# 64-row key transposes, and the first half of the attention step in another order

## The chip, the cores and the metric

The kernel runs on one core of a Trainium2 chip. The metric is the time of one execution on the device, in microseconds (us). The core's engines are TensorE (PE, its weight loads PEld), VectorE (DVE), ScalarE (ACT), GpSimd (POOL) and SyncE (SP), which here only issues DMAs. Each engine runs its own list of instructions in order, and semaphores tie the lists together.

## The reference

`x` and `ctx_4096` are (32, 64, 512): 32 batches, 64 channels, 512 positions. A linear cross attention comes first, then a feed-forward layer with 4-bit weights.

```python
qh = einsum('bcn,oc->bon', layernorm(x), Wq)    # 8 heads of 64
kh = einsum('bcn,oc->bon', ctx, Wk)
vh = einsum('bcn,oc->bon', ctx, Wv)
qh = softmax(qh, axis=-2) * SCALE               # over a head's 64 features
kh = softmax(kh, axis=-1)                       # over the 512 positions
context = einsum('bhdn,bhen->bhde', kh, vh)
out = einsum('bhde,bhdn->bhen', context, qh)
out = einsum('bcn,oc->bon', out.reshape(b, 512, -1), Wo) + bo
x = x + tanh(g_xattn) * (out / max(norm(out, axis=1), 1e-12) * g * sqrt(64))
x = x + tanh(g_ffn) * ffn(layernorm(x))         # gate, up and down products
```

## The kernel before

The attention works on pairs of batches: 16 pairs, two times 64 channels on the 128 partitions. The loop is a software pipeline of steps p = 0 to 17. In step p the logits and exponentials of pair p are made ("project"), the denominators and the context of pair p-1 ("combine"), and the output, its norm and the residual of pair p-2 ("residual"). Steps 0, 1, 16 and 17 do a part of this; 16 and 17 are the drain, where the feed-forward's input is transposed too. The steps are written out by hand, one list for each engine, and semaphores are counted by pair. The feed-forward layer (lines from 1097 on) comes after it and isn't touched.

TensorE's list in a full step has two halves. The first: `t_logits(t)` (query logits with n on the partitions, only for the row maxima, L625), `k_logits(t)` (L646), `denominators` (L679), `output` (L663), `context(t)` (L691: the transposed context input ctxT times the transposed key exponentials ekT, into the bank small[0]), `squared_norms` (L702), `q_max_rows` (transposes of the row maxima, L715) and `fold_context` (L726, also into small[0]). The second half is four rounds t = 0 to 3 of `spread_reciprocals(t)` (L743), `q_logits(t)` (L761 three times, then L763, which subtracts the maxima; all into k_pair) and `k_transposed(t)` (L776: 128 positions of all key exponentials ek are transposed into act_pair). `ctx_transposed` (L786) stands in round 0, `spread_inverse_norm` (L797) in round 2.

Who waits for whom around the change:

- ScalarE empties the banks in order. In a round it does the exponential of the query logits (L493, semaphore q_exp), then the copy of the transposed keys to ekT (L489, kt_evac). `q_logits(t)` waits for q_exp of round t-1, since both use k_pair; `k_transposed(t)` waits for kt_evac of round t-1.
- In the first half ScalarE does the key exponentials (L484, two for each t, after DVE's minimum L982), y and ysq (L501, L502), xs_hi (L452), ss_rows (L510), kctxT (L506, the context product out of small[0]; semaphore a_evac), qmax_rows (L555) and ctxT (L563; ct_evac).
- `fold_context` waits for a_evac. VectorE does the maxima (L979, L982), the reciprocals L991, and in the second half the products eq (L987).

A matmul's stationary operand fills rows x columns of the array. A row of the profile shows this as "64*128" or "128*128", and the moving operand behind it. "pair" is any of dve_pair, k_pair and act_pair, "small" either of small[0] and small[1].

## Time and profile before

| what | value |
|---|---|
| time, median of 3 runs | 786.22 us (785.8 to 786.3) |
| the profiled execution's own time | 788.89 us |
| its span | 787.1 us |
| TensorE, VectorE, ScalarE, GpSimd busy | 93%, 76%, 55%, 23% |
| mean granted TensorE clock | 0.974 of full speed |

The profiled execution took 2.67 us more than the median of the runs, of which 1.8 us lie outside its span. Times in the rows are counted from the start of the span. A row of the timeline gives a start, a duration up to the end of the last instruction merged into it, the engine, the line, and how many were merged; an idle time before it and its releaser follow in brackets. Matmuls are pipelined, so the duration of a row reaches beyond the start of the next one, and start to start is what a row costs. The attention steps fill the first 459 us or so, the feed-forward layer the rest.

### The profile page before, as it was taken

The numbers are of one execution on the slowest core, as the hardware profiler recorded it, in microseconds if no ns is written. First come the engines' busy times: TensorE is split into PE (matmuls) and PEld (weight loads), VectorE is DVE, ScalarE is ACT, GpSimd is POOL, SyncE is SP. The second block draws the span as 40 slices with busy tenths as digits, with TensorE's granted clock in tenths as the row PEclk, the third lists the DMA queues.
The fourth block names the chain that finished last, engine by engine and source line by source line (L and its number), as shares of the span: only waits on it lengthen the run. The fifth ranks groups of instructions, "written<-read, shape, count | busy, mean of one in ns | idle before, by whom it ended". The sixth has DMA issues, their size and how long they took to land. (4 is left out here: it accounts for less than half of the span.)

```text
span 787.1 us, 13752 instructions
## 1 busy us (share of the span) xinstructions
PE 732.0 (93%) x4551; PEld 395.1 (50%) x4551; DVE 594.7 (76%) x806; ACT 436.3 (55%) x764; POOL 179.5 (23%) x317
## 2 busy tenths in 40 slices
PE   4789999999999999999999754799999999999997
PEld 3445554565456545654565331254555455554555
DVE  6356878887888788778876463699988878877885
ACT  3657776677667767776776421354443344445333
POOL 5221222222222222222241112112121111111221
PEclk9999999999999999999999956799999999999999
DMA  3003303330233012202200000200001000100101
GB/s 102 28 5 84 81 13 85 85 85 11 80 82 84 19 58 69 71 16 61 70 20 7 4 4 1 75 1 0 1 2 40 15 0 13 40 0 0 40 13 54
DMA packets 29195, 29.89 MB, mean 38 GB/s; under 512 B 18628, under 2 KB 18756, under 8 KB 29036
## 3 DMA queue, kind: packets, MB, share of 16 engines
q1 hardware_dynamic: 26972, 28.85, 13.3%
q10 hardware_dynamic: 2192, 0.66, 0.3%
q8 instruction: 16, 0.26, 0.1%
q14 instruction: 15, 0.12, 0.1%
HBM read 23.49 MB, written 4.23 MB: 35 GB/s over the span
## 5 line engine op out<-in xcount | busy, mean ns | idle before, releaser
L1303 DVE SCALAR_TENSOR_TENSOR acc<-ffn_bank,scale_T,acc 128x512 f32<-128x512 f32 (+1 forms) x264 | 186.6, 747 | 39.6 <-PE ffn_bank L1256 34.1
L1255 PE MATMUL ffn_bank<-ek,w_gu 128*128 (+3 forms) x352 | 137.8, 392 | 3.0 <-PEq L90 1.8
L1256 PE MATMUL ffn_bank<-ekT,w_gu 128*128 (+3 forms) x352 | 134.1, 381 | 0.0
L987 DVE TENSOR_TENSOR eq<-eq,pair 128x1024 f32<-128x1024 f32 x64 | 78.1, 1221 | 65.8 <-PE pair L743 65.8
L1163 POOL TENSOR_TENSOR in_lo<-inter,in_hi 128x512 fp32r<-128x512 f32 (+1 forms) x44 | 56.4, 1283 | 229.8 <-ACT in_hi L1202 229.8
L1195 ACT ACTIVATE act_gate<-acc 128x512 f32<-128x512 f32 (+1 forms) x44 | 27.7, 631 | 144.3 <-DVE acc L1303 144.3
L484 ACT ACTIVATE ek<-pair,kneg 128x512 f32<-128x512 f32 x128 | 86.7, 686 | 8.2 <-DVE kneg L982 7.8
L1272 PE MATMUL ffn_bank<-wd_hi,in_hi 128*128 128x512 f32 (+1 forms) x176 | 86.7, 531 | 0.4 <-DVE wd_lo L1336 0.4
L979 DVE TENSOR_REDUCE qmax<-pair 128x16 f32<-128x1024 f32 x64 | 77.6, 1212 | 12.4 <-PE pair L625 12.2
L1272 PE MATMUL ffn_bank<-wd_lo,in_hi 128*128 128x512 f32 (+1 forms) x176 | 86.7, 531 | 0.0
L493 ACT ACTIVATE eq<-pair 128x1024 f32<-128x1024 f32 x64 | 65.7, 1026 | 30.5 <-PE pair L763 30.5
L1255 PEld LDWEIGHTS ffn_bank<-ek,w_gu 128*128 128x128 bf16 (+1 forms) x352 | 34.8, 99 | 91.8 <-issue 48.3
L982 DVE TENSOR_REDUCE kneg<-pair 128x2 f32<-128x1024 f32 x64 | 77.8, 1215 | 1.4 <-PE pair L646 1.4
L1272 PE MATMUL ffn_bank<-wd_hi,in_lo 128*128 128x512 f32 (+1 forms) x176 | 77.5, 479 | 0.1
L776 PE MATMUL pair<-ident,ek 128*128 128x128 f32 x512 | 70.8, 282 | 0.0
L776 PEld LDWEIGHTS pair<-ident,ek 128*128 128x128 f32 x512 | 55.5, 142 | 23.6 <-issue 16.9
L489 ACT ACTIVATE ekT<-pair 128x1024 f32<-128x1024 f32 x64 | 65.7, 1027 | 0.9 <-PE pair L776 0.9
L691 PE MATMUL small<-ekT,ctxT 128*64 128x512 f32 x256 | 62.4, 610 | 0.8 <-ACT den L497 0.8
L663 PE MATMUL small<-eq,fold 128*64 128x512 f32 x256 | 60.7, 618 | 2.1 <-ACT ekT L489 1.1
L1187 ACT ACTIVATE acc<-ffn_bank,scale_T 128x512 f32<-128x512 f32 (+1 forms) x88 | 58.5, 684 | 2.6
L349 POOL TENSOR_TENSOR rn_sq<-ss_max,minus_half 128x8 f32<-128x8 f32 x16 | 26.6, 1663 | 114.8 <-DVE ss_max L1025 114.8
L359 POOL TENSOR_TENSOR cs_lo<-ctx_raw,cs_hi 128x512 fp32r<-128x512 f32 x16 | 20.5, 1280 | 129.8 <-ACT cs_hi L448 129.7
(138 smaller groups left out, 1147.0 us busy)
## 6 DMA issues: line engine op xcount, KB each, us to landing
xall<-in_x SPq DMA_DIRECT2D x16, 256.0 KB, 2.7
ctx_raw<-in_ctx SPq DMA_DIRECT2D x16, 256.0 KB, 2.9
out_x<-xall SPq DMA_DIRECT2D x16, 256.0 KB, 2.0
zero<-zeros_plus SPq DMA_DIRECT2D x8, 344.0 KB, 4.3
packed<-in_L_ffn_gate_qweight SPq DMA_DIRECT2D x4, 688.0 KB
packed<-in_L_ffn_up_qweight SPq DMA_DIRECT2D x4, 688.0 KB
packed<-in_L_ffn_down_qweight SPq DMA_DIRECT2D x10, 256.0 KB
d_scale<-in_L_ffn_down_scales SPq DMA_DIRECT2D x1, 1408.0 KB, 6.2
```

What stands on the lines that cost most here:

```text
L484: act.activation(ek[:, b, t, :], k_pairs[t % 2][:, b, :], ACT.Exp, bias=kneg[:, b, t:t + 1], scale=-1.0, accum_out=ksum[:, k_slot(b, t):k_ ...
L489: act.activation(ekT[:, t, :, :], act_pair[:, :, :], ACT.Copy).then_inc(kt_evac, 1)
L493: act.activation(eq[:, par, t, :, :], k_pair[:, :, :], ACT.Exp).then_inc(q_exp, 1)
L691: last = pe.matmul(small[0][half(b), :], ctxT[:, t, half(b)], ekT[:, t, b, :], start=(t == 0), stop=(t == NT - 1))
L776: last = pe.transpose(act_pair[:, b, ot * P:(ot + 1) * P], ek[:, b, ot, t * P:(t + 1) * P], ident[:, :])
L979: dve.tensor_reduce(qmax[:, t, :, 0:HEADS], dve_pair[:, :, :].rearrange("n b (h d) -> n b h d", d=DH), AX.X, ALU.max).then_inc(t_max, 1)
L982: dve.tensor_reduce(kneg[:, :, t], k_pairs[t % 2][:, :, :], AX.X, ALU.min).then_inc(k_max, 1)
L987: dve.tensor_tensor(e, e, dve_pair[:, :, :], ALU.mult).then_inc(q_norm, 1)
L1255: pe.matmul(gu_bank[job % 4][0:w, :], lhsT, xT_hi[:, g, rows], start=True, stop=False)
L1256: pe.matmul(gu_bank[job % 4][0:w, :], lhsT, xT_lo[:, g, rows], start=False, stop=True).then_inc(gu_mm, 1)
L1272: ins = pe.matmul(y_bank[t][:, :], left, right, start=(it == 0 and kind == 0), stop=(it == IT - 1 and kind == 2))
L1303: dve.scalar_tensor_tensor(out=acc[0:w, it % 3, m, :], in0=gu_bank[job % 4][0:w, :], scalar=scale_T[0:w, it, 4 * m + g:4 * m + g + 1], in1 ...
```

## The change

Four edits.

1. `k_transposed` no longer transposes eight blocks of 128 rows but sixteen of 64 rows, in eight pairs: rows 0 to 63 into bank 0 of act_pair, rows 64 to 127 into bank 1. ekT so has another order of columns, and `context` reads it in runs of 64 numbers. `spread_inverse_norm` uses 64 rows instead of 128.
2. On TensorE `context(0)` to `context(3)` stand together behind `k_logits(2)`; before, `t_logits(3)`, `k_logits(3)` and `squared_norms` stood between the two halves.
3. `ctx_transposed` moves from round 0 of the second half to just ahead of `q_max_rows`, and from bank small[1] to small[0]. It now waits for a_evac, and `fold_context` waits for ct_evac of the same step.
4. ScalarE's list follows: y and ysq behind the key exponentials of t = 1, ss_rows behind kctxT, and ctxT ahead of qmax_rows. The wait for the last key exponentials moves from `k_transposed(0)` to the last matmuls of `q_logits(0)`.

```diff
--- before.py
+++ after.py
@@ -539,18 +539,20 @@
                     denominators()
                 k_exp_tile(0, 0)
                 k_exp_tile(0, 1)
+                k_exp_tile(1, 0)
+                k_exp_tile(1, 1)
                 if residual:
                     outputs()
-                k_exp_tile(1, 0)
-                k_exp_tile(1, 1)
                 if not last:
                     x_high(p + 1, 1 - par)
-                if residual:
-                    squared_norms()
                 k_exp_tile(2, 0)
                 k_exp_tile(2, 1)
                 if combine:
                     context()
+                if residual:
+                    squared_norms()
+                act.wait_ge(ct_mm, p + 1)
+                act.activation(ctxT[:, :, :].rearrange("n t c -> n (t c)"), small[0][:, :], ACT.Copy).then_inc(ct_evac, 1)
                 act.wait_ge(qmaxT_mm, p + 1)
                 act.activation(qmax_rows[:, :], small[1][:, :], ACT.Copy).then_inc(qmaxT_evac, 1)
                 k_exp_tile(3, 0)
@@ -558,10 +560,6 @@
                 for t in range(NT):
                     q_exp_tile(t)
                     k_transposed(t)
-                    if t == 0:
-                        act.wait_ge(ct_mm, p + 1)
-                        act.activation(ctxT[:, :, :].rearrange("n t c -> n (t c)"), small[1][:, :],
-                                       ACT.Copy).then_inc(ct_evac, 1)
 
             def transposed(first, end):
 
@@ -656,7 +654,7 @@
                         if at_least(p, 3):
                             pe.wait_ge(yn_ready, r - 1)
                         if not drain or combine:
-                            pe.wait_ge(ct_evac, r + 1)
+                            pe.wait_ge(qmaxT_evac, r + 1)
                         else:
                             pe.wait_ge(ss_evac, r - 1)
                     for b in range(2):
@@ -673,6 +671,7 @@
                         pe.wait_ge(yn_ready, r - 1)
                     if isinstance(p, int) and p == 1:
                         pe.wait_ge(pool_consts, POOL_CONSTS)
+                        pe.wait_ge(ct_evac, 1)
                     for tt in range(2):
                         for grp in range(4):
                             b, t = grp // 2, 2 * (grp % 2) + tt
@@ -688,8 +687,9 @@
                         pe.wait_ge(ct_evac, r + 1)
                         pe.wait_ge(d_evac, r + 1)
                     for b in range(2):
-                        last = pe.matmul(small[0][half(b), :], ctxT[:, t, half(b)], ekT[:, t, b, :],
-                                         start=(t == 0), stop=(t == NT - 1))
+                        heads = ekT[:, t, :, b * OT * DH:(b + 1) * OT * DH].rearrange("n e (t d) -> n t e d", d=DH)
+                        last = pe.matmul(small[0][half(b), :].rearrange("c (t e d) -> c t e d", t=OT, e=2),
+                                         ctxT[:, t, half(b)], heads, start=(t == 0), stop=(t == NT - 1))
                     if t == NT - 1:
                         last.then_inc(a_mm, 1)
 
@@ -710,7 +710,7 @@
                     if residual:
                         pe.wait_ge(ss_evac, r)
                     elif combine:
-                        pe.wait_ge(ct_evac, r + 1)
+                        pe.wait_ge(qmaxT_evac, r + 1)
                     for t in range(NT):
                         last = pe.transpose(small[1][:, t * P:(t + 1) * P],
                                             qmax[:, t, :, :].rearrange("n b h -> n (b h)"), ident[:, :])
@@ -720,6 +720,8 @@
                     if not combine:
                         return
                     pe.wait_ge(a_evac, r + 1)
+                    if project:
+                        pe.wait_ge(ct_evac, p + 1)
                     for b in range(2):
                         for t in range(OT):
                             for e in range(2):
@@ -759,6 +761,8 @@
                     for n, (w, v) in enumerate(((wqT_hi, xs_hi), (wqT_lo, xs_hi), (wqT_hi, xs_lo))):
                         for b in range(2):
                             pe.matmul(k_pair[:, b, :], w[half(b), cols], v[half(b), par, :], start=(n == 0), stop=False)
+                    if t == 0:
+                        pe.wait_ge(k_exp, 8 * p + 8)
                     for b in range(2):
                         last = pe.matmul(k_pair[:, b, :], minus_spread[half(b), t, :], qmax_rows[half(b), :],
                                          start=False, stop=True)
@@ -767,23 +771,24 @@
                 def k_transposed(t):
                     if not project:
                         return
-                    if t == 0:
-                        pe.wait_ge(k_exp, 8 * p + 8)
-                    else:
+                    pe.wait_ge(pool_consts, 2)
+                    if t > 0:
                         pe.wait_ge(kt_evac, 4 * p + t)
-                    for b in range(2):
-                        for ot in range(OT):
-                            last = pe.transpose(act_pair[:, b, ot * P:(ot + 1) * P], ek[:, b, ot, t * P:(t + 1) * P],
-                                                ident[:, :])
+                    for slot in range(2 * OT):
+                        b, ot = divmod(slot, OT)
+                        for e in range(2):
+                            last = pe.transpose(act_pair[:, e, slot * DH:(slot + 1) * DH],
+                                                ek[half(e), b, ot, t * P:(t + 1) * P], ident[half(e), half(e)])
                     last.then_inc(kt_mm, 1)
 
                 def ctx_transposed():
                     if not project:
                         return
                     pe.wait_ge(loaded[par], 32 * (i + 1))
-                    pe.wait_ge(qmaxT_evac, p + 1)
+                    if combine:
+                        pe.wait_ge(a_evac, r + 1)
                     for t in range(NT):
-                        last = pe.transpose(small[1][:, t * P:(t + 1) * P], ctx_raw[:, par, t * P:(t + 1) * P], ident[:, :])
+                        last = pe.transpose(small[0][:, t * P:(t + 1) * P], ctx_raw[:, par, t * P:(t + 1) * P], ident[:, :])
                     last.then_inc(ct_mm, 1)
 
                 def spread_inverse_norm():
@@ -794,7 +799,7 @@
                         pe.wait_ge(m_evac, r + 1)
                     else:
                         pe.wait_ge(yn_ready, r - 1)
-                    pe.matmul(small[0][:, :], spread_batch[:, :], rn_rows[:, :], start=True, stop=True).then_inc(rn_mm, 1)
+                    pe.matmul(small[0][:, :], spread_batch[0:C, :], rn_rows[0:C, :], start=True, stop=True).then_inc(rn_mm, 1)
 
                 def ffn_input(*tiles):
 
@@ -861,17 +866,17 @@
                 k_logits(2)
                 context(0)
                 context(1)
+                context(2)
+                context(3)
                 t_logits(3)
                 k_logits(3)
                 squared_norms()
-                context(2)
-                context(3)
+                ctx_transposed()
                 q_max_rows()
                 fold_context()
                 spread_reciprocals(0)
                 q_logits(0)
                 k_transposed(0)
-                ctx_transposed()
                 spread_reciprocals(1)
                 q_logits(1)
                 k_transposed(1)
```

TensorE, first half of step 2 (the steps in the loop have the same rows), before: from the last piece of `k_logits(2)` to `fold_context`; ctxT is the transposed context input, ysq the squared output, qmax the row maxima.

```order
L691 MATMUL small<-ekT,ctxT 64x512 x4
L625 MATMUL pair<-wqT_hi,xs_hi 128x512 x2
L646 MATMUL pair<-cs_hi,wkT_hi 128x512 x2
L646 MATMUL pair<-cs_hi,wkT_lo 128x512 x2
L646 MATMUL pair<-cs_lo,wkT_hi 128x512 x2
L702 MATMUL small<-ysq,batch_sum 32x128 x4
L691 MATMUL small<-ekT,ctxT 64x512 x4
L715 MATMUL small<-ident,qmax 128x128 x4
L726 MATMUL small<-foldT,kctxT 64x64 x16
L743 MATMUL pair<-rden_rows,spread 128x512 x2
```

The same place in the changed kernel.

```order
L691 MATMUL small<-ekT,ctxT 64x512 x8
L623 MATMUL pair<-wqT_hi,xs_hi 128x512 x2
L644 MATMUL pair<-cs_hi,wkT_hi 128x512 x2
L644 MATMUL pair<-cs_hi,wkT_lo 128x512 x2
L644 MATMUL pair<-cs_lo,wkT_hi 128x512 x2
L702 MATMUL small<-ysq,batch_sum 32x128 x4
L791 MATMUL small<-ident,ctx_raw 128x128 x4
L715 MATMUL small<-ident,qmax 128x128 x4
L728 MATMUL small<-foldT,kctxT 64x64 x16
L745 MATMUL pair<-rden_rows,spread 128x512 x2
```

The context product is one block of eight now, and the transposes of ctx_raw stand between the squared norms and those of qmax.

TensorE, second half, round 0 of step 2, before: from the last matmuls of the query logits to the spread of round 1.

```order
L763 MATMUL pair<-qmax_rows,minus_spread 128x512 x2
L776 MATMUL pair<-ident,ek 128x128 x8
L786 MATMUL small<-ident,ctx_raw 128x128 x4
L743 MATMUL pair<-rden_rows,spread 128x512 x2
L761 MATMUL pair<-xs_hi,wqT_hi 128x512 x2
```

The same place in the changed kernel, beginning with the products ahead of it.

```order
L763 MATMUL pair<-xs_lo,wqT_hi 128x512 x2
L767 MATMUL pair<-qmax_rows,minus_spread 128x512 x2
L780 MATMUL pair<-ident,ek 128x64 x16
L745 MATMUL pair<-rden_rows,spread 128x512 x2
L763 MATMUL pair<-xs_hi,wqT_hi 128x512 x2
```

The transposes of ctx_raw are gone from the round, and the key transposes are sixteen matmuls with 64 moving columns.

ScalarE, first half of a step in the loop, before: from y to the row maxima.

```order
L501 ACTIVATE y<-small,bo_col 128x512
L502 ACTIVATE ysq<-small,bo_col 128x512
L480 REGISTER_ALU
L484 ACTIVATE ek,ksum<-pair,kneg 128x512 x2
L451 REGISTER_ALU
L452 ACTIVATE xs_hi<-xn 128x512
L510 ACTIVATE ss_rows<-small 128x128
L480 REGISTER_ALU
L484 ACTIVATE ek,ksum<-pair,kneg 128x512 x2
L506 ACTIVATE kctxT<-small 128x512
L554 REGISTER_ALU
L555 ACTIVATE qmax_rows<-small 128x512
```

The changed kernel, from the key exponentials of t = 1, which now stand ahead of y, to ctxT; qmax_rows is the row after these.

```order
L484 ACTIVATE ek,ksum<-pair,kneg 128x512 x2
L500 REGISTER_ALU
L501 ACTIVATE y<-small,bo_col 128x512
L502 ACTIVATE ysq<-small,bo_col 128x512
L451 REGISTER_ALU
L452 ACTIVATE xs_hi<-xn 128x512
L480 REGISTER_ALU
L484 ACTIVATE ek,ksum<-pair,kneg 128x512 x2
L506 ACTIVATE kctxT<-small 128x512
L510 ACTIVATE ss_rows<-small 128x128
L554 REGISTER_ALU
L555 ACTIVATE ctxT<-small 128x512
```

ss_rows no longer stands ahead of the key exponentials of t = 2 but behind kctxT, and ctxT has come in behind it.

## Rows read from the trace of the kernel before

**Rows 1.** The page, parts 1 and 2: TensorE's busy time; its granted clock in 40 slices.
```profile
PE 732.0 (93%) x4551; PEld 395.1 (50%) x4551; DVE 594.7 (76%) x806; ACT 436.3 (55%) x764; POOL 179.5 (23%) x317
...
PEclk9999999999999999999999956799999999999999
```

**Rows 2.** Stretches: busy time (x count) of PE, PEld, DVE, ACT, POOL; clock; DMA.
```profile
300.00:400.00 100.00, 99.44 (x772) 53.57 (x768) 79.33 (x100) 69.84 (x128) 24.06 (x49) 1.00 0.21 57
460.00:480.00 20.00, 13.53 (x53) 6.60 (x53) 10.88 (x17) 4.80 (x9) 3.16 (x12) 0.60 0.01 1
```

**Rows 3.** Timeline of TensorE, second half of a middle step, rounds 0 to 2.
```profile
242.87 0.39 PE L763 MATMUL pair<-qmax_rows,minus_spread 64*128 64x512 f32 x2
243.19 1.09 PE L776 MATMUL pair<-ident,ek 128*128 128x128 f32 x8
244.12 0.60 PE L786 MATMUL small<-ident,ctx_raw 128*128 128x128 f32 x4
244.65 0.51 PE L743 MATMUL pair<-rden_rows,spread 64*128 64x512 f32 x2
...
247.37 0.40 PE L761 MATMUL pair<-xs_hi,wqT_hi 64*128 64x512 f32 x2
...
248.07 0.40 PE L763 MATMUL pair<-qmax_rows,minus_spread 64*128 64x512 f32 x2
```

**Rows 4.** Lines 591, 599 (transposes of weights) and 604: duration min/median/max, starts.
```profile
L591 PE MATMUL pair<-ident,ekT x4: 421/421/447, 6.8 to 7.5; 128*128 128x128 f32 x4
```
```profile
L599 PE MATMUL pair<-ident,ekT x4: 311/311/364, 9.3 to 9.7; 64*128 64x64 f32 x4
```
```profile
L604 PE MATMUL pair<-woT,ekT x16: 417/418/472, 10.9 to 12.4; 64*128 64x64 f32 x16
```

**Rows 5.** Timeline of ScalarE: the last exponential of one step to that of the next.
```profile
224.96 1.03 ACT L493 ACTIVATE eq<-pair 128x1024 f32<-128x1024 f32 x1 [0.57 <-PE pair L763]
...
239.08 0.69 ACT L484 ACTIVATE ek<-pair,kneg 128x512 f32<-128x512 f32 x1
...
240.09 0.60 ACT L506 ACTIVATE kctxT<-small 128x512 f32<-128x512 f32 x1 [0.23 <-PE small L691]
...
243.30 1.03 ACT L493 ACTIVATE eq<-pair 128x1024 f32<-128x1024 f32 x1 [0.69 <-PE pair L763]
...
246.12 1.03 ACT L493 ACTIVATE eq<-pair 128x1024 f32<-128x1024 f32 x1 [0.29 <-PE pair L763]
...
248.51 1.03 ACT L493 ACTIVATE eq<-pair 128x1024 f32<-128x1024 f32 x1 [0.35 <-PE pair L763]
...
251.12 1.03 ACT L493 ACTIVATE eq<-pair 128x1024 f32<-128x1024 f32 x1 [0.57 <-PE pair L763]
```

**Rows 6.** Timeline of step 0, TensorE and then ScalarE (no spread in it).
```profile
38.42 0.40 PE L763 MATMUL pair<-qmax_rows,minus_spread 64*128 64x512 f32 x2
```
```profile
38.86 1.02 ACT L493 ACTIVATE eq<-pair 128x1024 f32<-128x1024 f32 x1 [0.28 <-PE pair L763]
...
41.18 1.02 ACT L493 ACTIVATE eq<-pair 128x1024 f32<-128x1024 f32 x1 [0.28 <-PE pair L763]
```

**Rows 7.** Timeline of TensorE, first half of the same middle step.
```profile
234.70 1.94 PE L691 MATMUL small<-ekT,ctxT 128*64 128x512 f32 x8
...
237.75 0.43 PE L702 MATMUL small<-ysq,batch_sum 128*32 128x128 f32 x8
238.11 1.94 PE L691 MATMUL small<-ekT,ctxT 128*64 128x512 f32 x8
...
240.75 1.15 PE L726 MATMUL small<-foldT,kctxT 128*64 128x64 f32 x32
```

**Rows 8.** Timeline of VectorE, the minimum that the key exponentials of t = 2 wait for.
```profile
236.49 1.22 DVE L982 TENSOR_REDUCE kneg<-pair 128x2 f32<-128x1024 f32 x1
```

**Rows 9.** Step 1: TensorE's timeline, and the stretch that follows (columns as in rows 2).
```profile
52.81 0.79 PE L625 MATMUL pair<-wqT_hi,xs_hi 64*128 64x512 f32 x2 [2.75 <-DVE qmax L979]
```
```profile
52.80:56.20 3.40, 3.39 (x12) 1.69 (x14) 3.35 (x3) 1.45 (x4) 0.90 (x1) 0.50 0.07 14
```

## The prediction, made before the changed kernel had run

> **What bounds the kernel now.** I read the page first. TensorE is busy 93% of the span at nearly full clock, and its clock falls in one place only, in the middle, where the attention drains into the feed-forward layer [rows 1]. The table of stretches says the same of the steps: from 300 to 400 us TensorE is busy 99.4 of 100 us at clock 1.00, VectorE 79 and ScalarE 70 [rows 2]. So a step looks bound by TensorE alone. A step lasts 26.16 us (the last exponential starts at 224.96, the next step's at 251.12 [rows 5]), and there are 14 full ones.
>
> A busy share doesn't tell what comes next behind TensorE, so I went to the timelines of one step. The reader should see a second chain there, a ping-pong between two engines over one buffer: the query logits of a round wait until ScalarE has emptied k_pair with the exponential of the round before. The exponential of round 1 starts at 246.12 and ends at 247.15 [rows 5]. The first product of round 2 starts at 247.37 and the last at 248.07 [rows 3]; the next exponential starts at 248.51 [rows 5]. Only 0.22 us lie between the exponential's end and the logits. Step 0, which has no spread, shows that chain bare: the last product of its logits starts at 38.42, the exponential at 38.86, and the next one at 41.18 [rows 6]. The period is 2.32 us, and nothing but logits, exponential and transposes is in it. In a full step the three intervals between exponentials are 2.82, 2.39 and 2.61 us [rows 5], little above 2.32. This is the number on which my forecast rests.
>
> **The change, part by part.**
>
> *Key transposes.* Before, eight blocks start at 243.19 and the next work at 244.12: 0.93 us, of which about 0.06 waits for the first weights, so 0.109 each. Four more take 0.53 up to the spread at 244.65, 0.44 and 0.09 over [rows 3]. The new form isn't in this trace in pairs, but both bounds are. Line 599 is a transpose of 64 rows with 64 moving columns: four starts from 9.3 to 9.7, so some 0.12 apart. That is at half speed: the 128-row transposes of line 591 start from 6.8 to 7.5, some 0.22 apart [rows 4], twice the later 0.109. So it is 0.06 at full speed. Sixteen one after the other would be 0.9 us, as much as before. Line 604 has pairs of 64 rows with 64 moving columns and full products: eight pairs start from 10.9 to 12.4, 0.21 a pair, 0.107 at full speed [rows 4], and again 8 x 0.107 = 0.86. If the pairs overlap as the pairs of line 761 do (three pairs in 0.70 us, 0.233 each, the time of one [rows 3]), it is 8 x 0.055 = 0.44. I take 0.46, since pairs are what the change issues; by all of these it is no dearer than about 0.9.
>
> *Changes of shape.* From the last 64*128 products at 242.87 to the transposes there are 0.32 us where a pair costs 0.233: 0.09 for changing from 64*128 to 128*128. The way back costs 0.09 again, and each time the first weight load is bare, 0.06 and 0.11 [rows 3]. That is 0.35 us for each block of transposes, and it goes away, since now all of the round is 64*128. The Trainium skill, "TensorEngine Tiling (Array Packing)", section Key Properties, says that changing the tiling mode drains TensorE; the trace agrees with 0.09 each way. By that rule alone, with TensorE as the bound, the change would be worth what rival 1 says.
>
> *What a round costs then.* TensorE's own work is 0.23 (spread) + 0.93 (logits) + 0.46 = 1.62 us instead of 2.39. But the ping-pong stays: exponential 1.03, logits to the last product 0.70 + 0.40, the rest waits for semaphores and the first load. With 0.86 for the transposes TensorE's work would be 2.02, still under 2.32, so the speed of the transposes doesn't decide. The three intervals shrink from 2.82 + 2.39 + 2.61 = 7.82 to 3 x 2.32 = 6.96: **-0.86 us a step**. ctx_transposed (0.44 of the first interval) and the inverse norm (0.23 of the last) are in this. VectorE's product (1.22, with 0.87 of weight unpacking in two of the rounds) fits into 2.32.
>
> *The first half.* The context product stands in one piece. Its second half starts at 238.11 and moves to behind the first, which starts at 234.70; eight rows take about 1.72 [rows 7]. So `squared_norms` goes from 237.75 to 239.47, and what follows it 0.36 later starts at 239.8. `ctx_transposed` now also waits for ScalarE's kctxT. That comes after the key exponentials of t = 2, which wait for VectorE's minimum, at 236.49 + 1.22 = 237.71 [rows 8]: 237.75, two at 0.67, then kctxT from 239.09 to 239.70. It was at 240.09 before [rows 5]. TensorE can transpose at 239.8, four in 0.60, so 240.40; ScalarE copies ctxT to 241.04; `fold_context` waits for that and starts at 241.09, where before it started at 240.75 [rows 7]. Everything up to the exponential of round 0 comes 0.34 us later: **+0.34 us**. ScalarE then has qmax_rows and two key exponentials, to 242.9, before the exponential at 243.64; so it isn't late itself. Moving y, ysq and ss_rows takes a wait for TensorE out of the way of the key exponentials, but these wait for VectorE, so I cost it at nothing; if VectorE were earlier it would gain.
>
> *Sum.* 0.34 - 0.86 = -0.52 us a step, 14 steps: -7.3. Step 1 has more: TensorE waits 2.75 us for the row maxima ahead of `t_logits(3)`, and the clock is 0.50 in the stretch behind it [rows 9]. The whole context product now stands ahead of that wait and fills it, and I estimate that `fold_context` comes 0.75 earlier; with the second half -1.6. Step 0 loses in its first half (four transposes, at half clock) and gains in its round 1; I estimate -0.4. The total is -9.3 us, against 788.9 of the profiled execution 779.6. The median of the runs is 2.67 lower: **777 us**, 1.2% faster. The drain and the feed-forward layer keep their times.
>
> **Rivals.**
> 1. TensorE stays the bound and the ping-pong gives way. Per step 4 x (2.39 - 1.62) = 3.1 us; 14 steps and a part of two, some -48 us: 738. Step 0 speaks against it [rows 6]. In between: the first half costs nothing and the rounds are as I say, -0.86 x 14 - 2 = -14: 772. Chance of anything under 773: 0.12.
> 2. The other side: `context` reads its moving operand in runs of 64 numbers with jumps, no row shows that, and nothing hides it, since `fold_context` hangs on it. The block is 16 rows at 0.215, 3.44 us [rows 7]. If each took f times as long, the step gets 3.44 (f - 1) longer, and from f = 1.15 on the gain is gone. At the price that 1.3 would have: +0.5 us a step, 793. Chance 0.07.
> 3. The first half stretches more than 0.34, since on ScalarE and TensorE kctxT, ss_rows, ctxT and qmax_rows form one chain of four mutual waits, and small[0] now has four uses in a row. With 0.3 more for each step: -3 to -5 us, 782; with 0.6 more, no change, 786; more than that, slower. Chance 0.13 for 781 to 784.6, 0.09 for no change, 0.04 for slower.
> 4. Sixteen weight loads where there were eight. If each costs what a 128-row one does (at most 0.109 [rows 3]) and they don't overlap, a block takes 1.74, a round 2.9, and the step gets about 2 us longer: 815. Line 599 shows half of that for 64 rows [rows 4]. Chance 0.02. The Trainium skill, "TensorE: Matmul & The Clock Gate", section LDWEIGHTS, states that a load's time goes by columns and not by rows, P / 1.2 ns, 107 ns for these; that is an estimate from the page, and by it the loads alone give this rival unless pairs overlap.
> 5. TensorE, idle 0.7 of 2.32 us in each round, loses clock. In the drain it is busy 13.5 of 20 us at clock 0.60 [rows 2]. Its work of 1.62 a round would double: +3.6 us a step, 835. Against it, the idle times here are 0.5 us and those of the drain several times as long, and step 0 idles without losing it. Chance 0.03.
>
> **How the numbers follow.** My forecast (773 to 781) has 0.50. Under 773 is rival 1, 0.12; 781 to 784.6 0.13; within 0.2% (784.6 to 787.8, about what a measurement of this kernel can tell from no change) 0.09; above it rivals 2 to 5, 0.07 + 0.04 + 0.02 + 0.03 = 0.16. Faster: 0.50 + 0.12 + 0.13 = 0.75. The range of 8 in 10 leaves out most of rival 1 and the dear ends of rivals 2, 4 and 5: 769 to 788.
>
> **What the profile will show.** Right: intervals between the exponentials of L493 of about 2.32 us, TensorE waiting for ScalarE ahead of the logits by some 0.5 us a round, transposes in a block of 0.4 to 0.9 us with no gap around, `fold_context` 0.3 us later relative to the first `k_logits`, and a step of 25.6 us; TensorE busy under 90%. Wrong: a step under 25 us would mean that another chain than the ping-pong ruled; a context block of more than 3.6 us is rival 2; a clock under 1.00 from 100 to 400 us is rival 5.

## The result, and the profile after

The changed kernel takes 788.94 us (median of 18 runs, 788.1 to 791.4), the kernel before in the same sessions 786.78 (18 runs, 785.8 to 789.3): a ratio of 1.0026, interval 1.0015 to 1.0036. It is slower by 0.26%, where I had said 777 us and 1.2% faster. The executions of before gather near 786.2 and near 788.6, those of after near 788.6 and 791.2, and the profiled execution of before (788.89, span 787.1) is one of its upper group, that of after (789.32, span 787.5) one of its lower. So the two traces stand only 0.4 us apart. The steps below are compared within the two traces. By how much traces can differ in step 1 with the same instructions is told below, under "Steps 0 and 1".

The page after, parts 1 and 2, beside [rows 1]; then the group of the key transposes (count, busy us, mean ns, idle us ahead of it).
```profile
PE 708.1 (90%) x5063; PEld 382.5 (49%) x5063; DVE 595.1 (76%) x806; ACT 432.0 (55%) x764; POOL 185.8 (24%) x317
...
PEclk9999999999999999999999956799999999999999
```
```profile
L780 PE MATMUL pair<-ident,ek 64*128 64x64 f32 x1024 | 45.8, 224 | 0.0
```

TensorE has lost 24 us of busy time and the span has lost none. The stretch of [rows 2], after:
```profile
300.00:400.00 100.00, 94.18 (x882) 51.13 (x880) 78.17 (x100) 68.97 (x129) 25.11 (x49) 1.00 0.20 57
```

TensorE idles 5.8 us of 100 instead of 0.6, at the same clock of 1.00. The next fence is ScalarE's timeline of a middle step, beside [rows 5].
```profile
224.23 1.02 ACT L493 ACTIVATE eq<-pair 128x1024 f32<-128x1024 f32 x1 [1.02 <-PE pair L767]
...
237.62 0.68 ACT L484 ACTIVATE ek<-pair,kneg 128x512 f32<-128x512 f32 x1
238.28 0.59 ACT L506 ACTIVATE kctxT<-small 128x512 f32<-128x512 f32 x1
...
239.14 0.28 ACT L510 ACTIVATE ss_rows<-small 128x128 f32<-128x128 f32 x1 [0.26 <-PE small L702]
...
239.69 0.60 ACT L555 ACTIVATE ctxT<-small 128x512 f32<-128x512 f32 x1 [0.28 <-PE small L791]
...
242.99 1.02 ACT L493 ACTIVATE eq<-pair 128x1024 f32<-128x1024 f32 x1 [0.83 <-PE pair L767]
...
245.31 1.02 ACT L493 ACTIVATE eq<-pair 128x1024 f32<-128x1024 f32 x1 [0.37 <-PE pair L767]
...
247.63 1.02 ACT L493 ACTIVATE eq<-pair 128x1024 f32<-128x1024 f32 x1 [0.38 <-PE pair L767]
...
250.62 1.02 ACT L493 ACTIVATE eq<-pair 128x1024 f32<-128x1024 f32 x1 [1.05 <-PE pair L767]
```

Read the starts of L493. Two of the three intervals are the 2.32 us that I forecast (242.99, 245.31, 247.63). The third is 2.99, longer than the 2.61 of before, and from the last exponential of one step to the first of the next there are 18.76 us instead of 18.34. The table sums the pieces for the middle steps; the last row holds for those that unpack weights of 128x688.

| | first half and logits(0) | interval 1 | 2 | 3 | step |
|---|---|---|---|---|---|
| before | 18.3 | 2.82 | 2.39 | 2.61 | 26.1 |
| forecast | 18.6 | 2.32 | 2.32 | 2.32 | 25.6 |
| after | 18.8 | 2.32 | 2.32 | 2.96 to 2.99 | 26.4 |

TensorE's timeline in round 2 shows where the third interval goes.
```profile
247.43 0.69 PE L780 MATMUL pair<-ident,ek 64*128 64x64 f32 x16
248.92 0.50 PE L802 MATMUL small<-rn_rows,spread_batch 64*128 64x512 f32 x1 [0.80 <-DMA rn_rows<-rn_parts]
249.01 0.64 PE L745 MATMUL pair<-rden_rows,spread 64*128 64x512 f32 x2
249.35 0.53 PE L763 MATMUL pair<-xs_hi,wqT_hi 64*128 64x512 f32 x2
```

`spread_inverse_norm` (L802) stands in TensorE's list ahead of `spread_reciprocals(3)` and `q_logits(3)`. It waits 0.80 us for a DMA, and everything behind it waits too. The table of waits has this 15 times in the kernel; a row gives the sum, the count and the longest, in us. The second row is the same wait before.
```profile
PEld small L802 <- DMA rn_rows<-rn_parts: 15.7, 15, 3.9
```
```profile
PEld small L797 <- DMA rn_rows<-rn_parts: 3.9, 1, 3.9
```
The one wait of 3.9 us is there in both. New are 14 waits, one for each full step, 11.8 us together.

To see why rn_rows is late, follow its makers backwards: SyncE issues the DMA (L302), GpSimd makes rn_parts (L349 to L353), VectorE makes ss_max (L1030). First VectorE of the changed kernel, then GpSimd, then SyncE.
```profile
243.20 0.17 DVE L1030 TENSOR_SCALAR ss_max<-ss_sq 128x8 f32<-128x8 f32 x1
243.88 1.22 DVE L992 TENSOR_TENSOR eq<-eq,pair 128x1024 f32<-128x1024 f32 x1
245.02 0.87 DVE L975 TENSOR_TENSOR w_gu<-packed,zero 128x688 int32 x1
```
```profile
245.17 0.78 POOL L351 TENSOR_TENSOR rn_parts<-rn_sq,ones 128x8 fp32r<-128x8 f32 x1
```
```profile
246.26 1.19 SPq L302 DMA_DIRECT2D rn_rows<-rn_parts  x2
```

And the same places in the kernel before.
```profile
243.51 0.17 DVE L1025 TENSOR_SCALAR ss_max<-ss_sq 128x8 f32<-128x8 f32 x1
...
245.19 1.22 DVE L987 TENSOR_TENSOR eq<-eq,pair 128x1024 f32<-128x1024 f32 x1 [0.93 <-PE pair L743]
246.33 0.87 DVE L970 TENSOR_TENSOR w_gu<-packed,zero 128x688 int32 x1
```
```profile
245.48 0.20 POOL L351 TENSOR_TENSOR rn_parts<-rn_sq,ones 128x8 fp32r<-128x8 f32 x1
```
```profile
246.00 1.19 SPq L302 DMA_DIRECT2D rn_rows<-rn_parts  x2
```

In both, VectorE's product of round 1 is followed by the unpacking of 4-bit weights (L975, before L970). Round 0 has lost ctx_transposed, so the product starts 0.68 us behind ss_max instead of 1.68, and the unpacking now begins 0.15 us before GpSimd's copy L351 instead of 0.85 behind it. The copy takes 0.78 us instead of 0.20, and the DMA is issued 0.26 later, although ss_max was 0.31 earlier. TensorE asks for the rows at 248.12 (248.92 less the 0.80 of idle time), where before it came to them at 249.25 and found them there. Counted from the exponential of round 0 (243.30 before, 242.99 after), the issue moved from 2.70 to 3.27 us and the use from 5.95 to 5.13.

### The profile page after: what moved, and what is told of

Same layout as the page of the kernel before. It is cut to its first block and busy times, and to the rows that moved or that the text cites. A ratio compares the mean times of both kernels' runs of the same rounds, so it can differ in the third digit from the quotient of the medians.

```text
span 787.5 us, 14838 instructions
## 1 busy us (share of the span) xinstructions
PE 708.1 (90%) x5063; PEld 382.5 (49%) x5063; DVE 595.1 (76%) x806; ACT 432.0 (55%) x764; POOL 185.8 (24%) x317
## 5 line engine op out<-in xcount | busy, mean ns | idle before, releaser
L984 DVE TENSOR_REDUCE qmax<-pair 128x16 f32<-128x1024 f32 x64 | 77.8, 1215 | 27.6 <-PE pair L623 27.4
L493 ACT ACTIVATE eq<-pair 128x1024 f32<-128x1024 f32 x64 | 65.6, 1025 | 39.3 <-PE pair L767 39.3
L987 DVE TENSOR_REDUCE kneg<-pair 128x2 f32<-128x1024 f32 x64 | 77.9, 1217 | 1.7 <-PE pair L644 1.6
L661 PE MATMUL small<-eq,fold 128*64 128x512 f32 x256 | 60.6, 617 | 2.5 <-ACT ekT L489 1.5
L691 PE MATMUL small<-ekT,ctxT 128*64 128x512 f32 x256 | 58.5, 598 | 0.8 <-ACT den L497 0.8
L349 POOL TENSOR_TENSOR rn_sq<-ss_max,minus_half 128x8 f32<-128x8 f32 x16 | 26.6, 1661 | 132.0 <-DVE ss_max L1030 132.0
L780 PEld LDWEIGHTS pair<-ident,ek 64*128 64x128 f32 x1024 | 43.2, 138 | 10.2 <-issue 7.5
L780 PE MATMUL pair<-ident,ek 64*128 64x64 f32 x1024 | 45.8, 224 | 0.0
```

Source lines behind the costliest of these rows:

```text
L493: act.activation(eq[:, par, t, :, :], k_pair[:, :, :], ACT.Exp).then_inc(q_exp, 1)
L661: last = pe.matmul(small[1][half(b), :], fold[:, k_slot(b, t), :], eq[:, par, t, b, :], start=(t == 0), stop=(t == OT - 1))
L780: last = pe.transpose(act_pair[:, e, slot * DH:(slot + 1) * DH], ek[half(e), b, ot, t * P:(t + 1) * P], ident[half(e), half(e)])
L984: dve.tensor_reduce(qmax[:, t, :, 0:HEADS], dve_pair[:, :, :].rearrange("n b (h d) -> n b h d", d=DH), AX.X, ALU.max).then_inc(t_max, 1)
L987: dve.tensor_reduce(kneg[:, :, t], k_pairs[t % 2][:, :, :], AX.X, ALU.min).then_inc(k_max, 1)
```

## The experiments

Ratios are to the kernel before, in the same sessions. The intervals are read from ScalarE's timeline, as above. Where an experiment starts from "the transposes alone", that is the second one.

### The inverse norm behind the last logits

```diff
--- after.py
+++ inverse_norm_later.py
                 k_transposed(2)
-                spread_inverse_norm()
                 spread_reciprocals(3)
                 q_logits(3)
+                spread_inverse_norm()
                 k_transposed(3)
```

> The changed kernel with one line moved: the product that spreads the inverse norm stands behind the query logits of round 3, no longer ahead of that round's spread. Theory L (the late rows of the inverse norm hold up round 3 of the second half, 2.99 us between exponentials where the others have 2.32): the interval of round 3 falls to 2.32, the others stay, a step of the gate and up weights goes from 26.38 to about 25.7 us, and the time to 778 to 780 us, 1% faster than before. Rival V (VectorE, with a product of 1.22 and an unpacking of 0.87 us in a round, holds up the spread of round 3): the interval stays at 2.9, and so does the time, 789.

Measured: 780.21 us (779.3 to 780.5), ratio 0.9895 [0.9879, 0.9911]. The last exponentials of a step, ScalarE:
```profile
244.62 1.02 ACT L493 ACTIVATE eq<-pair 128x1024 f32<-128x1024 f32 x1 [0.37 <-PE pair L767]
...
246.93 1.03 ACT L493 ACTIVATE eq<-pair 128x1024 f32<-128x1024 f32 x1 [0.37 <-PE pair L767]
```
The third interval is 2.31 and the step 25.68, close to the 25.6 that I had forecast for the change itself, and the time is just above the 778 to 780 that I expected here. From the last exponential of step 1 to that of step 15 there are 359.85 us instead of the 365.92 of before: 6.1 less, where I had forecast 7.3. GpSimd's copy still takes 0.77; it only no longer matters. One matmul's place in TensorE's list is worth 8.7 us between this and the changed kernel, and the sign of the result hangs on it.

### The transposes alone

The kernel before with the 64-row transposes, their order of columns in `context`, the 64-row inverse norm and the moved wait for the last key exponentials; the order of the first half stays.

```diff
--- before.py
+++ transposes_alone.py
-                        last = pe.matmul(small[0][half(b), :], ctxT[:, t, half(b)], ekT[:, t, b, :],
+                        heads = ekT[:, t, :, b * OT * DH:(b + 1) * OT * DH].rearrange("n e (t d) -> n t e d", d=DH)
...
-                    for b in range(2):
-                        for ot in range(OT):
-                            last = pe.transpose(act_pair[:, b, ot * P:(ot + 1) * P], ek[:, b, ot, t * P:(t + 1) * P],
-                                                ident[:, :])
+                    for slot in range(2 * OT):
+                        b, ot = divmod(slot, OT)
+                        for e in range(2):
+                            last = pe.transpose(act_pair[:, e, slot * DH:(slot + 1) * DH],
+                                                ek[half(e), b, ot, t * P:(t + 1) * P], ident[half(e), half(e)])
```

> The kernel before with the 64-row transposes alone (the new column order in the context product and the 64-row inverse norm go with them), all else in the old order. Theory L: intervals 2.4 to 2.5, 2.32 and 2.8 us, first half as before at 18.3, a step of 25.9 us and a time of about 783 us. Rival F (the first half's new order is harmless, and the transposes carry the loss): 788 or more. Rival P (TensorE's share rules, as in my first rival): a step under 25 us, 765.

Measured: 774.92 us (772.7 to 776.5), ratio 0.984 [0.9823, 0.9857], the fastest kernel of this study together with the one that adds the later norm. ScalarE:
```profile
235.13 1.03 ACT L493 ACTIVATE eq<-pair 128x1024 f32<-128x1024 f32 x1 [0.70 <-PE pair L766]
...
237.58 1.03 ACT L493 ACTIVATE eq<-pair 128x1024 f32<-128x1024 f32 x1
...
239.90 1.02 ACT L493 ACTIVATE eq<-pair 128x1024 f32<-128x1024 f32 x1 [0.38 <-PE pair L766]
...
242.21 1.02 ACT L493 ACTIVATE eq<-pair 128x1024 f32<-128x1024 f32 x1 [0.37 <-PE pair L766]
```
I had expected the third interval to stay at about 2.8 and the time at about 783, and missed both: the interval is 2.31. With ctx_transposed still in round 0 the first interval is 2.45 and the unpacking starts 0.48 us behind the copy, which takes 0.20 again:
```profile
237.31 0.20 POOL L351 TENSOR_TENSOR rn_parts<-rn_sq,ones 128x8 fp32r<-128x8 f32 x1
```
```profile
237.79 0.87 DVE L973 TENSOR_TENSOR w_gu<-packed,zero 128x688 int32 x1
```
```profile
240.45 0.49 PE L800 MATMUL small<-rn_rows,spread_batch 64*128 64x512 f32 x1
```
From the copy's start to the inverse norm there are 3.14 us and no wait; in the changed kernel 3.75 and a wait. The rows come just in time here: the DMA is issued at 237.83, and the 2.62 us to the inverse norm are no more than in kernels that wait for it. So the transposes by themselves don't make the copy slow.

### The order alone

The changed kernel with the old 128-row transposes, the old reading in `context` and the 128-row inverse norm (the second diff's "+" lines back to its "-" lines).

> The changed kernel with the 128-row transposes, the old column order and the 128-row inverse norm back: the new order alone. Theory L: first half 18.75 us as in the changed kernel, intervals 2.4, 2.4 and 3.0, a step of 26.5 us, and 790 to 792 us, slower than before. Rival F: first half near 18.3 and a time at or under that of before, 782 to 786.

Measured: 788.25 us (12 runs), ratio 1.0006 [0.9992, 1.0019]. The first half takes 18.81 us, the intervals are 2.39, 2.37 and 2.61, the copy takes 0.20. I had expected a third interval of 3.0 and 790 to 792 us, and missed: there is no wait for rn_rows here. What ctx_transposed gives back in interval 1 (0.43) pays for what the first half loses (0.5). So the transposes give 1.6% by themselves, the order nothing, and both together -0.26%: they do not add.

The start of VectorE's unpacking against that of GpSimd's copy shows why. Before, it comes 0.85 us behind the copy. The transposes alone bring it to 0.48 behind (237.79 and 237.31), the order alone to 0.42 behind (247.05 and 246.63), and a copy of 0.20 us is over by then. Both together bring it to 0.15 ahead. So the slow copy is a product of neither part, it takes both.

### The unpacking in one piece

Only VectorE's list changes: the first piece of unpacking no longer stands behind the product of round 1.

```diff
--- after.py
+++ unpacking_in_one_piece.py
-                    if weights:
-                        less_zero(p, *weights, 0)
                     normalise(2)
...
                     if weights:
+                        less_zero(p, *weights, 0)
                         less_zero(p, *weights, 1)
```

> The changed kernel with VectorE's first piece of weight unpacking moved from behind the product of round 1 to behind that of round 2, next to the second piece. GpSimd's copy of the inverse norm takes 0.78 us in the changed kernel and 0.20 before; it now lies beside that unpacking. Theory G (VectorE's unpacking holds GpSimd up, and this is most of why the inverse norm is late): the copy is back at 0.20, the last interval falls from 2.99 to about 2.45, a step to 25.8, and the time to some 781 us. Rival: the copy stays at 0.78, or the wait stays for another reason, time 789.

Measured: 783.5 us (781.6 to 784.8), ratio 0.9934 [0.9917, 0.9951]. GpSimd, then TensorE:
```profile
243.36 0.20 POOL L351 TENSOR_TENSOR rn_parts<-rn_sq,ones 128x8 fp32r<-128x8 f32 x1
```
```profile
246.50 0.50 PE L802 MATMUL small<-rn_rows,spread_batch 64*128 64x512 f32 x1 [0.21 <-DMA rn_rows<-rn_parts]
```
The copy is back at 0.20 us, the wait falls from 0.80 to 0.21, and the interval from 2.96 to 2.41 on average. I had expected 2.45 and some 781 us. This ties the slow copy to the unpacking beside it, with TensorE's list untouched. It also parts the 0.80 us in two: about 0.6 is the copy, 0.2 would be there in any case.

### The context product whole

The transposes alone, plus edits 2 and 4 without ctx_transposed's: `context` in one piece, and y, ysq and ss_rows later in ScalarE's list.

```diff
--- transposes_alone.py
+++ context_whole.py
                 k_exp_tile(0, 1)
-                if residual:
-                    outputs()
                 k_exp_tile(1, 0)
                 k_exp_tile(1, 1)
+                if residual:
+                    outputs()
...
-                if residual:
-                    squared_norms()
                 k_exp_tile(2, 0)
...
                     context()
+                if residual:
+                    squared_norms()
...
                 context(1)
+                context(2)
+                context(3)
                 t_logits(3)
                 k_logits(3)
                 squared_norms()
-                context(2)
-                context(3)
```

> The 64-row transposes (the kernel of transposes alone) plus the context product in one piece and ScalarE's new order, with the transposes of ctx_raw still in round 0. Theory C (of the 0.54 us that the new order adds to the first half, nearly all comes from the chain kctxT, transposes of ctx_raw, ctxT, fold): first half 18.3 us, at most 0.1 over the 18.23 of the transposes alone, intervals as there, time 775 to 777. Rival W (the context product in one piece delays the row maxima and the last key exponentials): first half 18.7 and 782 or more.

Measured: 776.83 us (774.9 to 778.6), ratio 0.9855 [0.9831, 0.988]. The first half takes 18.50 us where the transposes alone take 18.26 (means of the full steps). I had expected 0.1 more at most. TensorE:
```profile
234.07 0.63 PE L716 MATMUL small<-ident,qmax 128*128 128x128 f32 x4 [0.49 <-ACT ss_rows L510]
234.63 1.15 PE L727 MATMUL small<-foldT,kctxT 128*64 128x64 f32 x32
```
`q_max_rows` waits 0.49 us for ss_rows, since both use small[1], and ss_rows now stands behind kctxT on ScalarE. So the new order of ScalarE's list, which I had costed at nothing, has a price: with the context product whole it is 0.24 us a step. That ss_rows' place makes it is read from this wait; no run moved ss_rows by itself.

### The transposes of ctx moved, the context product split

The transposes alone, plus edit 3 and its part of edit 4 (ctxT ahead of qmax_rows).

```diff
--- transposes_alone.py
+++ ctx_transposes_moved.py
                 squared_norms()
                 context(2)
                 context(3)
+                ctx_transposed()
                 q_max_rows()
                 fold_context()
                 spread_reciprocals(0)
                 q_logits(0)
                 k_transposed(0)
-                ctx_transposed()
```

> The 64-row transposes plus the transposes of ctx_raw moved ahead of the row maxima's, into the bank of the context product, with the context product still in two pieces. Theory C: the chain now begins when the second piece ends, so fold comes 1.2 to 1.4 us later than with the transposes alone; first half 19.5, first interval 2.32 instead of 2.44, a step of about 26.5 and a time of 792. Rival W: first half about 18.3, time 773 to 776.

Measured: 803.59 us (801.6 to 804.7), ratio 1.02 [1.0173, 1.0227]; I had expected 792. The first half takes 19.77 us. TensorE:
```profile
248.29 0.63 PE L791 MATMUL small<-ident,ctx_raw 128*128 128x128 f32 x4 [0.79 <-ACT kctxT L506]
...
249.70 1.15 PE L728 MATMUL small<-foldT,kctxT 128*64 128x64 f32 x32 [0.34 <-ACT ctxT L555]
```
The chain that I had worked out for the changed kernel (context product, kctxT, transposes, ctxT, `fold_context`) is bare here: 0.79 and 0.34 us of idle time. The first half is 1.51 longer than with the transposes alone. With the context product whole the same move costs 0.28 (18.78 less 18.50). So edit 2 is what makes edit 3 bearable, and what I expected of each by itself was too small (at most 0.1 and some 1.3, for 0.24 and 1.51). The rest of the miss is in the third interval: it is 2.94 to 3.00 in the steps that unpack 128x688, with the copy at 0.78 as in the changed kernel, where I had expected a step of 26.5 and got 27.4.

### The transposes alone with the later norm

The first experiment's edit on the transposes alone.

> The transposes alone, with the spread of the inverse norm moved behind the query logits of round 3 as in the first experiment. Theory L says that this helps only where the rows come late: with the old order the intervals are at 2.32 already, so no change against the transposes alone, 773 to 777. If it gained 5 us as it did in the changed kernel (9 us), the late rows wouldn't be what it cured.

Measured: 774.97 us (774.0 to 775.8), ratio 0.9837 [0.9814, 0.9861]; the first half 18.26, the intervals 2.44, 2.32, 2.31. No change against the transposes alone: there TensorE doesn't wait for rn_rows, so nothing is to be had.

### The changed kernel with 128 rows in the inverse norm

`spread_inverse_norm` alone goes back to 128 rows (a single run, 792.78).

> The changed kernel with the inverse norm's product on 128 rows again. In the changed kernel the second matmul of each pair in round 3 starts 0.13 to 0.14 us behind the first, where elsewhere it is some 3 ns; the 64-row product ahead occupies one half of the rows only. If that is the cause, the lag is gone here, two changes of shape come in, and the last interval stays between 2.9 and 3.1. If the lag stays, it has another cause.

The third interval is 3.17, more than the 2.9 to 3.1 that I had expected, so the 64 rows are worth 0.2 us to the changed kernel. TensorE:
```profile
251.87 0.50 PE L802 MATMUL small<-rn_rows,spread_batch 128*128 128x512 f32 x1 [0.77 <-DMA rn_rows<-rn_parts]
...
252.64 0.40 PE L763 MATMUL pair<-xs_hi,wqT_hi 64*128 64x512 f32 x2
```
The wait is nearly the same. From the inverse norm to the first logits there are 0.77 us instead of 0.43 (248.92 to 249.35). That fits the change of shape to 128*128 and back, which my second step had priced for the transposes, but no run shows it apart.

## Why the prediction was wrong, step by step

- **What bounds the kernel: right.** The ping-pong of ScalarE and TensorE over k_pair rules the rounds. In every kernel with the 64-row transposes the undisturbed intervals are 2.30 to 2.33 us. Step 0, which I took for the bare chain, could not show it before: TensorE is busy there itself, 3.90 of 4 us from 34 to 38 and from 38 to 42. After, it can: with an interval of 2.32 TensorE now waits 0.59 us in it.
```profile
35.69 0.50 PE L763 MATMUL pair<-xs_hi,wqT_hi 64*128 64x512 f32 x2 [0.59 <-ACT eq L493]
```
- **Key transposes, 0.46 us a block: right.** In round 0 the block starts at 242.79 and the spread behind it at 243.34, 0.55 with the change of moving data, in round 1 it is 0.48 (245.10 to 245.58); nothing is idle around it. Rivals 4 and 1 fall with it: loads overlap, and no full step came under 25.0 us.
- **What a round costs then, three intervals of 7.82 to 3 x 2.32 = 6.96, -0.86 us a step: the step that failed.** I said of the inverse norm only that its 0.23 us of work "are in this". I priced the instruction and not what it waits for. Measured are 2.32 + 2.32 + 2.96 = 7.60: of the 0.86 us that I forecast 0.22 remain. That the DMA was late is shown by the wait; that GpSimd's copy beside VectorE's unpacking makes 0.6 of the 0.8 us is shown by the unpacking in one piece; that this cost the forecast is shown by the later norm, whose ratio of 0.9895 is close to the 0.988 that I had forecast.
- **The first half, +0.34: right in its mechanism, too small.** Measured +0.47 (18.78 for 18.32, means of the full steps). Counted from the 18.26 of the transposes alone, 0.24 comes with the context product whole and ScalarE's order, 0.28 with the transposes of ctx. I had laid all of it on the second and costed y, ysq and ss_rows at nothing. What I said of kctxT was nearly exact: it starts at 238.28, at the end of its key exponentials, with no wait for TensorE any more.
- **Sum of a step, -0.52: wrong.** Measured +0.25 in the steps that unpack 128x688, where the copy takes 0.78 us, and +0.04 in those that unpack 128x512, where it takes 0.51 to 0.60 and the last interval is 2.75 to 2.82. From the end of step 1 to the end of step 15 it comes to +2.3 us, +0.16 a step, instead of -7.3.
- **Steps 0 and 1, -2.0: near in number, by luck.** The last exponential of step 0 starts at 39.25 instead of 41.18, that of step 1 at 66.00 instead of 68.26: -2.3. But -1.93 of it are in step 0, where I had -0.4, and only -0.33 in step 1, where I had -1.6. The context product does fill the wait for the row maxima in step 1, which falls from 2.75 to 1.04 us; then TensorE waits for the same ScalarE chain as in the other steps, and `fold_context` comes 0.25 earlier (16.70 us behind the last exponential of step 0 instead of 16.95), not 0.75.
```profile
50.89 0.50 PE L623 MATMUL pair<-wqT_hi,xs_hi 64*128 64x512 f32 x2 [1.04 <-DVE qmax L984]
...
54.08 1.09 PE L791 MATMUL small<-ident,ctx_raw 128*128 128x128 f32 x4 [2.00 <-ACT kctxT L506]
```
  Nor can one pair of traces show 2 us here. The changed kernel, the one with the later norm and the one with 128 rows in the inverse norm have the same instructions up to the end of step 1, and its last exponential starts at 66.00, 67.02 and 67.74. The transposes alone and the same with the later norm have the same ones too, and theirs at 64.83 and 67.46. TensorE idles 2.75 us ahead of `t_logits(3)` in both, and then its granted clock is 1.00 in the first and at the lower level, 0.50, in the second (columns as in [rows 2]):
```profile
53.00:56.00 3.00, 2.89 (x38) 1.50 (x36) 1.78 (x2) 2.45 (x7) 0.00 (x0) 1.00 0.03 5
```
```profile
53.00:56.00 3.00, 3.00 (x10) 0.77 (x8) 1.66 (x2) 0.88 (x4) 0.00 (x0) 0.50 0.02 5
```
  These two executions lie 3.2 us apart (772.65 and 775.81), though the medians of the two kernels agree, and 2.6 of it are there at the end of step 1. The trace of before has it at 0.50 as well. So the -2.3 is not the change's alone. What the change did is better read behind step 1: +2.3 us up to step 15, near the 2.2 between the medians.
- **Rival 2, the context product's reading in runs of 64 numbers: no cost.** Its sixteen rows go from 233.93 to the next start at 237.52, 3.59 us. The sixteen rows of `output` (L661), as many products of the same size that read plainly, go from 229.22 to 232.81 in the same trace, 3.59 too.
- **Rival 3, the first half stretches more than 0.34:** it did, by 0.13 a step, less than half of what that rival needed for 782. It doesn't explain the result: with the norm moved the same first half gives 780.2.
- **Rival 5, the clock:** out for the full steps, 1.00 from 300 to 400 us with TensorE 94% busy. Step 0, which I named against it, was no evidence, since TensorE hardly idles there before.
- **The rival that was missing** is the one that came: a transfer that had been hidden by slack, on TensorE's in-order list ahead of the work that sets the pace. [rows 3] hold the place in time, and no row that I had read the chain of rn_rows. Before, 3.25 us lie between the issue at 246.00 and the use at 249.25; after, TensorE goes on 2.66 us behind the issue (246.26 to 248.92). So there were 0.59 us of slack. The shorter rounds take 0.82 (5.95 less 5.13) and the later issue 0.57: 0.59 - 0.82 - 0.57 = -0.80, the wait that is there. Without the slow copy it would be -0.23, and the unpacking in one piece shows 0.21.

## What to carry to other kernels

When a change shortens the rounds ahead of an instruction, price what that instruction waits for and not just its work: write the slack of every DMA and every small result that stands on the busiest engine's list ahead of the bounding chain, and move such an instruction behind the work that sets the pace. Try the parts of a change apart: here one part alone gave 1.6%, the other nothing, and their sum a loss that one line undoes. And when work is moved on one engine, look which instructions of VectorE and GpSimd now run at the same time, above all those that read both their inputs from SBUF.

## What the runs showed of the hardware that was not expected

- **A small GpSimd copy beside VectorE's unpacking.** The copy of 128x8 numbers (L351) takes 0.20 us in the kernel before, beside VectorE's fp32 products, and 0.77 to 0.78 beside its subtraction on unpacked int32 weights of 128x688, 0.59 beside that of 128x512. The slow copy came and went with the unpacking: 0.77 to 0.78 in the changed kernel, with the later norm, with 128 rows in the inverse norm and with ctx_transposed moved alone; 0.20 in the order alone, in the three kernels that have the 64-row transposes and ctx_transposed in round 0, and with the unpacking in one piece. A step that unpacks 128x512 has the same, VectorE and then GpSimd in the changed kernel:
```profile
376.43 0.69 DVE L975 TENSOR_TENSOR d_int<-packed,zero 128x512 int32 x1
```
```profile
376.59 0.59 POOL L351 TENSOR_TENSOR rn_parts<-rn_sq,ones 128x8 fp32r<-128x8 f32 x1
```
  The copy ends at 377.18, 0.06 us behind the unpacking's end at 377.12; in the step shown first 245.95 and 245.89, 0.06 again. So it is not slowed by a share, it stands until the unpacking has ended. The Trainium skill, "SBUF — State Buffer", section Who interferes with whom, calls the pair of ports that the two engines share an exclusive lock, and says that an instruction of VectorE with two SBUF inputs contends with one of GpSimd that reads SBUF. The trace agrees for both lengths: both inputs of the unpacking are in SBUF. It says too that an instruction of VectorE with at most one SBUF input does not contend, outside its 2-port modes. The trace agrees for the product L987 of the kernel before (eq is in SBUF, pair is a PSUM bank): the copy of 0.20 us lies beside it. The ports themselves no run shows.
- **Pairs of 64-row transposes** cost 0.062 us from one pair to the next (the start of each matmul of the trace). The weight loads of one half of the rows start as close, less than the 107 ns that rival 4 names for one of them. Reading the moving operand in runs of 64 fp32 numbers costs nothing (rival 2 above).
- **A lone 64-row matmul puts pairs out of step.** Behind the 64-row inverse norm the second matmul of each pair of logits starts some 136 ns behind the first, in round 0 3 to 4 ns: the merged row of L763 at 249.35 lasts 0.53 us. With 128 rows in the inverse norm it lasts 0.40, as shown above. It did not decide anything here, since that kernel pays more for the change of shape.
